# Joined maxima for two key chunks of the odd heads, in a one-core block of attention, feed-forward and linear attention

## The reference, cut to what matters

```python
x = x + attn_a(layernorm(x), ...)      # 2 sequences of 2048 tokens, 256 features
x = x + ffn(layernorm(x), ...)
x = x + attn_b(layernorm(x), ...)
x = x + ffn(layernorm(x), ...)

# attn_a: 16 query heads, 4 key/value heads of 16 features, full softmax
scores = jnp.einsum('bghnd,bhsd->bghns', q, k)
attn = jax.nn.softmax(scores / SCALE, axis=-1)
out = jnp.einsum('bghns,bhsd->bghnd', attn, v)
return out @ Wo + bo
```

## Time and profile before

| | |
|---|---|
| median of 3 runs | 2197.43 us (2196.96 to 2198.44) |
| the profiled execution's own time | 2189.54 us |
| its span | 2187.7 us |
| busy: PE, DVE, ACT, POOL | 95%, 82%, 68%, 6% |
| attention steps with maxima | about 149 to 1398 us of the span |
| mean granted PE clock | 0.973 of full speed |

### The profile page before, as it was taken

How to read it: one execution, slowest core, us unless ns; L and a number is a source line. 1 busy time by engine, 2 the same in 40 slices (tenths; PEclk the granted TensorE clock), 3 DMA queues, 4 the chain that set the end, 5 groups by cost and what they waited for, 6 DMA issues and landing times.

```text
span 2187.7 us, 48018 instructions
## 1 busy us (share of the span) xinstructions
PE 2085.6 (95%) x14214; PEld 857.4 (39%) x14214; DVE 1784.7 (82%) x3349; ACT 1478.1 (68%) x2899; POOL 140.7 (6%) x210
## 2 busy tenths in 40 slices
PE   6899999999999999999999999898997999998997
PEld 3423333333333333333333333254434555555433
DVE  5689999999999999999999999644537677776255
ACT  4438888888888888888888888744556434446653
POOL 2350000000000000000000000010002000002000
PEclk9779999999999999999999999999997999999998
DMA  6421121121121221221221221230000000000002
GB/s 165 129 69 42 45 74 48 48 75 42 52 72 41 56 68 41 62 63 41 63 61 41 66 58 42 74 102 26 1 0 1 1 0 1 1 0 1 0 0 77
DMA packets 93686, 101.19 MB, mean 46 GB/s; under 512 B 35712, under 2 KB 74896, under 8 KB 93552
## 3 DMA queue, kind: packets, MB, share of 16 engines
q1 hardware_dynamic: 93552, 99.79, 16.8%
HBM read 78.72 MB, written 20.71 MB: 45 GB/s over the span
## 4 chain that ended last, share of the span: by engine, by line
PE 86%; DVE 6%; issue 3%; ACT 3%; DMA 1%; SPq 0%; ACTq 0%; POOL 0%; DVEq 0%; POOLq 0%
PE ps L613 22%; PE ps L587 14%; PE ps L636 10%; PE ps L642 10%; PE ps L743 8%; PE ps L751 4%; PE ps L553 3%; PE ps L819 2%; PE ps L828 2%; PE ps L848 2%; PE ps L602 1%; ACT YT L1001 1%; PE ps L764 1%; PE ps L532 1%; PE ps L867 1%
## 5 line engine op out<-in xcount | busy, mean ns | idle before, releaser
L1298 DVE TENSOR_REDUCE mx<-ps 128x1 f32<-128x512 f32 x2048 | 1279.4, 683 | 23.5 <-PE ps L587 18.8
L1001 ACT ACTIVATE YT<-ps 128x512 f32<-128x512 f32 x2048 | 1058.0, 606 | 273.8 <-PE ps L642 273.7
L613 PE MATMUL ps<-YT,work 128*32 128x512 f32 x4096 | 546.1, 605 | 0.0
L587 PE MATMUL ps<-work 64*128 64x512 bf16 x2048 | 461.3, 389 | 7.5 <-DVE mx L1298 6.9
L636 PE MATMUL ps<-work 64*128 64x512 bf16 x2048 | 406.0, 378 | 2.8
L642 PE MATMUL ps<-work 34*128 34x512 bf16 x2048 | 400.6, 378 | 0.0
L587 PEld LDWEIGHTS ps<-work 64*128 64x128 bf16 x2048 | 144.6, 93 | 613.0 <-DVE mx L1298 541.6
L636 PEld LDWEIGHTS ps<-work 64*128 64x128 bf16 x2048 | 162.0, 94 | 110.5 <-ACT YT L1001 36.3
L743 PE MATMUL ps<-YT,c_s 128*128 128x512 f32 x384 | 176.6, 603 | 3.2 <-ACT work L1050 2.5
L613 PEld LDWEIGHTS ps<-YT,work 128*32 128x32 f32 x4096 | 80.7, 108 | 123.0 <-issue 86.9
L642 PEld LDWEIGHTS ps<-work 34*128 34x128 bf16 x2048 | 101.1, 94 | 49.6 <-issue 1.7
(11 more groups left out here) (142 smaller groups left out, 1670.2 us busy)
## 6 DMA issues: line engine op xcount, KB each, us to landing
work<-k_scr SPq DMA_DIRECT2D x640, 64.0 KB, 2.2
work<-q_scr SPq DMA_DIRECT2D x640, 32.0 KB, 1.8
o_scr<-o_sb SPq DMA_DIRECT2D x32, 256.0 KB, 2.1
X<-in_L_attn_a_x_dram SPq DMA_DIRECT2D x8, 512.0 KB, 7.3
work<-negt SPq DMA_DIRECT2D x256, 1.0 KB
work<-o_scr SPq DMA_DIRECT2D x16, 256.0 KB
work<-inv_scr SPq DMA_DIRECT2D x16, 256.0 KB
out_dram<-X SPq DMA_DIRECT2D x16, 256.0 KB, 2.2
```

The source lines that it names most:

```text
L587: mm(ps[:, bank_of[x], :], qa[rows, p, jp, qt * P:(qt + 1) * P], ka[rows, p, kc_ * CH:(kc_ + 1) * CH], start=True, stop=True).then_inc(a_m ...
L613: m = mm(ps[32 * j:32 * j + 32, 7, :], vst[:, p, t, :], prob(GROUP * t + j), start=t == 0, stop=t == KTILES - 1)
L1001: fn(prob(u), ps[:, S_BANK + u % S_RING, :], ACT.Exp, scale=HD ** -0.5).then_inc(exp_ok, 1)
L1298: dve.tensor_reduce(mx[:, p, at_:at_ + 1], ps[:, bank_of[x], :], AX_X, ALU.max).then_inc(a_max, 1)
```

## The change: the key chunks 2 and 3 of the odd half share one pass on VectorE

For the odd half the loaded keys hold, in place of chunk 2, the difference of chunk 2 and chunk 3 (formed from float32 projections, split again in a high and a middle part, kept in the new scratch `d_scr`). So product x % 8 == 5 gives the difference of the two chunks' scores, and x % 8 == 7 the scores of chunk 3. ScalarE takes the positive part of the difference (`raised`, a Relu from PSUM into `above`), and VectorE adds it to the scores of chunk 3 and takes the maximum in one instruction (`tensor_tensor_reduce`). A step then has 56 VectorE passes in place of 64, and 8 Relus on ScalarE. The number of PE products and their order stay. PE waits for a Relu (`a_up`) where the bank held a difference.

```diff
-REDUCED = MAXU + 1
+SHARE = 2 * KC
+JOINED = MAXU // SHARE
+REDUCED = MAXU - JOINED + 1
...
+            def is_raised(x):
+                return x % SHARE == SHARE - 3
+            def is_joined(x):
+                return x % SHARE == SHARE - 1
+            def reduced_to(x):
+                return x + 1 - (x + 3) // SHARE
...  # PE, max_mm
-                wait(pe, a_max, REDUCED * s + after_of[x])
+                last = after_of[x]
+                if last == -4:
+                    wait(pe, a_up, JOINED * s)
+                elif last < 0:
+                    wait(pe, a_max, REDUCED * s + 1 + last)
+                elif is_raised(last):
+                    pe.wait_ge(a_up, JOINED * s + last // SHARE + 1)
+                else:
+                    pe.wait_ge(a_max, REDUCED * s + max(reduced_to(last), 1))
...  # ACT, the new helper, its places in a step
+            def raised(s, x):
+                act.wait_ge(a_mm, MAXU * s + x + 1)
+                if x >= 2 * SHARE:
+                    act.wait_ge(a_max, REDUCED * s + reduced_to(x + 2 - 2 * SHARE))
+                else:
+                    wait(act, a_max, REDUCED * (s - 1) + reduced_to(x + 2 + MAXU - 2 * SHARE))
+                act.activation(above[:, x // SHARE % 2, :], ps[:, bank_of[x], :], ACT.Relu).then_inc(a_up, 1)
...
                 for t in range(KTILES):
+                    x = AHEAD + GROUP * t + 1
+                    if is_raised(x) and x < MAXU and ahead >= 1:
+                        raised(s + 1, x)
+                    if is_raised(x) and x >= MAXU and ahead >= 2:
+                        raised(s + 2, x - MAXU)
                     for j in range(GROUP):
...  # ACT, chunks 6 and 7, in place of the loop over them
+            high(6, 0)
+            raised(0, 5)
+            put_row(0, 7, 0)
+            high(6, 1)
+            put_row(0, 7, 1)
+            raised(0, 13)
+            high(6, 2)
+            raised(0, 21)
+            raised(0, 29)
+            middle(6)
+            high(7, 0)
+            raised(0, 37)
+            high(7, 1)
+            high(7, 2)
+            raised(0, 45)
+            raised(0, 53)
+            raised(0, 61)
+            raised(1, 5)
+            raised(1, 13)
+            middle(7)
...  # ACT, middle
+                if c % CPG == CPG - 1:
+                    act.wait_ge(p_df, c // CPG + 1)
+                    if c >= CPG:
+                        act.wait_ge(d_st[0], 16 * 2)
+                    act.copy(part_d[:, 0, :], k_diff[:]).then_inc(p_dh, 1)
                 act.wait_ge(p_res, c + 1)
...
                 act.copy(part(c, 1), qkf(c)).then_inc(p_mid, 1)
+                if c % CPG == CPG - 1:
+                    act.wait_ge(p_ds, c // CPG + 1)
+                    act.copy(part_d[:, 1, :], k_diff[:]).then_inc(p_dm, 1)
...  # SP, store: the stores of d_scr
+                if pt < 2 and c4 != 2:
+                    sp.dma_start(d_scr[b * KV_HEADS:(b + 1) * KV_HEADS, pt, :, ch(c4)],
+                                 part(c, pt)[0:64, 2, :]).then_inc(k_st[pt][buffer_of(c)], 16)
+                if pt == 1 and c4 == CPG - 1:
+                    sp.wait_ge(p_dm, b + 1)
+                    for r in range(2):
+                        sp.dma_start(d_scr[b * KV_HEADS:(b + 1) * KV_HEADS, r, :, ch(2)], part_d[:, r, :]).then_inc(d_st[b], 16)
...  # DVE, maxima
-                    dve.wait_ge(a_mm, MAXU * s + x + 1)
-                    dve.tensor_reduce(mx[:, p, at_:at_ + 1], ps[:, bank_of[x], :], AX_X, ALU.max).then_inc(a_max, 1)
+                    if is_raised(x):
+                        continue
+                    at_ = place(x)
+                    if not is_joined(x):
+                        dve.wait_ge(a_mm, MAXU * s + x + 1)
+                    if is_joined(x + 1):
+                        dve.wait_ge(a_mm, MAXU * s + x + 2)
+                        dve.wait_ge(a_up, JOINED * s + x // SHARE + 1)
+                    if is_joined(x):
+                        dve.tensor_tensor_reduce(out=joined[:], in0=ps[:, bank_of[x], :], in1=above[:, x // SHARE % 2, :],
+                                                 scale=1.0, scalar=LOWEST, op0=ALU.add, op1=ALU.max,
+                                                 accum_out=mx[:, p, at_:at_ + 1]).then_inc(a_max, 1)
+                    else:
+                        dve.tensor_reduce(mx[:, p, at_:at_ + 1], ps[:, bank_of[x], :], AX_X, ALU.max).then_inc(a_max, 1)
...  # residue of chunk 3 (DVE) and of chunk 7 (POOL), around its own subtraction
+                    pool.wait_ge(p_kd, 2)
+                    pool.tensor_tensor(k_diff[:], k_diff[:], qkf(c)[0:KVD, 2, :], ALU.subtract).then_inc(p_df, 1)
...
+                    pool.wait_ge(p_dh, 2)
+                    pool.wait_ge(p_res, NCH)
+                    pool.tensor_tensor(k_diff[:], k_diff[:], part_d[:, 0, :], ALU.subtract).then_inc(p_ds, 1)
```

More of the change, by code:

```diff
@@ L58 @@
 S_BANK, S_RING = 3, 4
+LOWEST = -3.0e38
 GLOBAL_AT = (5, 9)
@@ L169, in hybrid_block @@
         mx = sb("mx", [P, 2, MAXU])
+        joined = sb("joined", [P, CH])
+        k_diff = sb("k_diff", [KVD, CH])
+        part_d = sb("part_d", [KVD, 2, CH], BF16)
         mxq = sb("mxq", [P, GROUP * QT])
@@ L212, in hybrid_block @@
         ka, qa = take(2, SEQ, dt=BF16), take(2, JP, CH, dt=BF16)
+        above = take(2, CH)
         def prob(u):
@@ L267, in hybrid_block @@
         x_ld = [sem(f"x_ld{c}") for c in range(NCH)]
+        d_st = [sem(f"d_st{b}") for b in range(BATCH)]
         def ch(c):
@@ L274, in kv_of, with place @@
             return s // (CPG * KV_HEADS) * KV_HEADS + s % KV_HEADS
+        def is_raised(x):
[4 more added lines that the diff above has]
+            return x + 1 - (x + 3) // SHARE
+        def place(x):
+            return (x % 2 * JP * QT + x // 2 // KC) * KC + x // 2 % KC
         bank_of, after_of = [], []
@@ L281, in hybrid_block @@
             bank_of.append(b_)
-            after_of.append(used[b_] + 1)
+            after_of.append(used[b_])
             used[b_] = x_
@@ L300, in buffer_of, with keys_stored @@
             return c // CPG * 2 + c % 2
+        def keys_stored(pt, c):
+            return (1, 1, 2, 2)[c % CPG] if pt == 2 else (2, 2, 3, 4)[c % CPG]
         def stored(eng, pt, c):
@@ L362, in load_queries, with load_keys @@
                                          q_scr[s, 2 * jp + g, 0:2].rearrange("r d n -> (r d) n")).then_inc(done[p], 16)
-            def load_keys(k_dst, p, s, done):
+            def load_keys(k_dst, p, s, done, odd):
                 for g in range(2):
@@ L368, in load_keys, with load_coarse @@
                         for part_row in (row, row + HD):
-                            sp.dma_start(k_dst[part_row:part_row + HD, p], k_scr[kv_of(s), r]).then_inc(done[p], 16)
-            def load_coarse(q_dst, k_dst, p, s, done):
+                            sp.dma_start(k_dst[part_row:part_row + HD, p], (k_scr, odd)[g][kv_of(s), r]).then_inc(done[p], 16)
+            def load_coarse(q_dst, k_dst, p, s, done, odd):
                 load_queries(q_dst, p, s, done)
-                load_keys(k_dst, p, s, done)
+                load_keys(k_dst, p, s, done, odd)
             def load_fine(p, s, done):
@@ L431, in _ @@
                     stored(sp, pt, c)
+            sp.wait_ge(d_st[1], 16 * 2)
             def next_maxima(s, p):
@@ L958, in high @@
                 fn(qkf(c)[:, n, :], ps[:, qk_bank(c, n), :], ACT.Identity, bias=b)
+                if n == 2 and c % CPG == 2:
+                    wait(act, p_dm, c // CPG)
+                    fn(k_diff[:], ps[0:KVD, qk_bank(c, n), :], ACT.Identity, bias=bias[0:KVD, BK:BK + 1]).then_inc(p_kd, 1)
                 fn(part(c, 0)[:, n, :], ps[:, qk_bank(c, n), :], ACT.Identity, bias=b).then_inc(p_act, 1)
             def middle(c):
+                if c % CPG == CPG - 1:
[3 more added lines that the diff above has]
+                    act.copy(part_d[:, 0, :], k_diff[:]).then_inc(p_dh, 1)
                 act.wait_ge(p_res, c + 1)
@@ L991, in collect, with step @@
                 act.copy(o_sb[:, p, :], ps[:, 7, :]).then_inc(o_ev, 1)
-            def step(i, p, before=True):
+            def step(i, p, before=True, ahead=2):
                 s = 2 * i + p
                 for t in range(KTILES):
+                    x = AHEAD + GROUP * t + 1
[3 more added lines that the diff above has]
+                        raised(s + 2, x - MAXU)
                     for j in range(GROUP):
@@ L1008, in _ @@
             step(1, 1)
-            with act.Fori(2, STEPS // 2) as i:
+            with act.Fori(2, STEPS // 2 - 1) as i:
                 step(i, 0)
                 step(i, 1)
+            step(STEPS // 2 - 1, 0, ahead=1)
+            step(STEPS // 2 - 1, 1, ahead=0)
             collect(STEPS - 1, STEPS // 2 - 1, 1)
@@ L1233, in residue @@
                 dve.wait_ge(p_act, 3 * (c + 1))
+                if c == CPG - 1:
+                    dve.wait_ge(p_kd, 1)
```

(5 more changed lines are left out.)

24 lines of the change are left out of this document (15 added, 9 removed).

## The result

The changed kernel takes 2213.8 us (median of 4 runs, 2211.91 to 2214.37) against 2197.23 us (median of 4; three of them gave the 2197.43 of the table): ratio 1.0074, 95% interval 1.0059 to 1.009, so 16.6 us slower. The forecast was +26.8.

A forecast was written before the change was run, and what follows sets the result against it. It took a loop of latencies between PE and VectorE, 2.48 us a unit, to bound the kernel. Passes 0, joined pass 0, odd Relus 0, boundaries 10.8 and start 16.0 gave +26.8 us, 2224 us; range 2206 to 2262.

The forecast's parts named there:

- The loop of latencies: Attention units: 2.48 us set by waits between PE and VectorE, kept in every unit; removed passes return 0.
- 35 us: Attention units: gain if the fourth product were not held, 0.07 us a unit, 2.41 us each, over 31 steps x 16 units.
- The closing units don't gain either: Two units closing a step's maximum: no gain, as their fourth product waits in the same order as now.
- The joined pass: VectorE in odd units: the add-and-maximum pass takes 0.60 us, up to 0.71 free; cost 0, upper end 122 us.
- rival C: VectorE's joined pass is longer than 0.71 us: +22 us at 0.80, +122 at 1.20; chance 0.22.
- The Relu in odd units: ScalarE in odd units: the Relu takes 0.49 us, covered by existing waits; cost 0, upper end 12 us.
- Rival D: ScalarE's Relu switches activation tables: 657 us more, 2880 us in all; chance 0.01.
- The start: Before the first step: middle(7) behind raised(1, 13) delays PE's first fine product from 148.46 to 164.5; +16.0 us, bounds +11 to +20.
- the extra work of the earlier chunks: Before attention: chunk 3's extra stores and casts fall where ScalarE waits; cost 0, upper end 2 us.
- The boundaries: Steps 1 to 30: Relu behind ScalarE's copy of the sums, 0.33 us each, 0.40 with a loop turn; 10.8 us, bounds 0 to 15.
- A: Attention units: VectorE's pace is the bound, units go to 2.41 us, 2189 us or 2173; chance 0.06.
- B: Only the step boundaries or only the start cost as read: 2208 to 2214 us; chance 0.16.

The follow-up runs named there:

- Experiments 2 and 3: Kernel before, each unit's fourth reduction (2) or first reduction (3) over 16 of 512 keys: 2182.86 us (ratio 0.9964) and 2145.54 us (0.9783).
- experiment 2: Kernel before, with each unit's fourth reduction over 16 of the 512 keys, 512 passes in all: 2182.86 us, ratio 0.9964.
- experiment 1: Changed kernel with middle(7) put ahead of raised(0, 61) in ScalarE's order: 2199.64 us, ratio 1.0037 against the kernel before.
- experiment 4: Experiment 1 plus the Relu of x = 21, behind the copy of the sums, over 16 of 512 columns: 2190.29 us, ratio 0.9994 against the kernel before.
- experiment 5: Kernel before, with ScalarE's loop over the steps 4 to 31 written out, nothing else: 2179.93 us, ratio 0.9936.
- experiments 1, 5 and 6: 1 and 5 as listed; 6 is experiment 1 with ScalarE's loop written out: 2188.51 us, ratio 0.9979 against the kernel before.

## Why the prediction was right

It said slower, by 26.8 us in the profiled execution, 2224 by the runs; it is +22.4 profiled and +16.6 by the runs, inside the range. Which of the two is nearer the truth is not told by these runs: the profiled execution of before lies 7.7 us below its own median, the changed one 1.9, so part of the gap is scatter.

**The loop of latencies: right.** Units of 2.48 us in both kernels, with 115 us less VectorE work in 1000. Experiments 2 and 3 show the mechanism and not only the outcome: 512 fourth passes made short gave 9.2 us, as many first ones 46.5, and only the second moved the load of the fourth product. For 35 us I had worked out 0.07 a unit; it is 0.07 (2.48 to 2.41) on the trace, that is 35 of the 46.5. The trace places the rest, roughly: three units of each step lasted 2.57, 2.61 and 2.65 us before and last 2.41 there too, which is 0.36 us a step or 11 us beyond; the first fine product comes 4.2 us earlier; and the turns of ScalarE's loop cost some 3.5 us more (3.74 for 3.47). One point was too strict: "The closing units don't gain either". A lighter VectorE did shorten the second one by 0.16 in experiment 2. In the changed kernel it did not, as the prediction said: there no pass between the two was removed.

**The joined pass: right.** The next pass begins 0.62 us behind it, the addition of the earlier trace rows had 0.60, and up to 0.71 was free. The mean duration in the groups, 681 ns, is the same as a plain reduction's. So rival C is out. The rule of the Trainium skill on half throughput that the prediction quotes stays untested, since one source here came from PSUM.

**The Relu in odd units: right, and no table load.** 0.50 us to the next exponential, units unchanged. Rival D is out by this row of ScalarE's groups:
```profile
L1137 ACT ACT_TABLE_LOAD x2 | 2.6, 1283 | 3.1 <-PE ps L789 3.1
```
The count is that of the earlier trace rows, with 256 Relus more in the kernel. The trace agrees with the rule quoted from the Trainium skill (ScalarE: Activation LUTs, Table sets).

**The start: the right step, 16.0 forecast, 19.8 measured at the first fine product.** The chain itself came in the order written, but later from its first link on: the middle part's cast at 151.32 against 148.3 (+3.0), the loads of the negated maxima at 161.88 against 157.6 (+4.3; SyncE waited 3.1 us for the stores to land, not 2.2), the product at 168.29 against 164.5 (+3.8). The last link was read wrongly: the 1.57 us from the end of the loads to the product is no landing time, as before the change PE was busy with lone maxima products until 148.06. Here it is 168.29 - 167.22 = 1.07. The part that was mis-sized most is the one costed at "0, upper end 2": the extra work of the earlier chunks, of which the prediction names chunk 3's alone. VectorE's first reductions in the changed kernel:
```profile
90.32 1.76 DVE L1326 TENSOR_TENSOR qkf_b<-qkf_b,part_b 128x1536 f32<-128x1536 f32 x1 [7.01 <-ACT part_b L1008]
...
96.35 2.47 DVE L1404 TENSOR_REDUCE mx<-ps 128x1 f32<-128x512 f32 x4
```
and in the kernel before:
```profile
86.87 1.76 DVE L1234 TENSOR_TENSOR qkf_b<-qkf_b,part_b 128x1536 f32<-128x1536 f32 x1 [6.94 <-ACT part_b L959]
...
92.89 2.47 DVE L1298 TENSOR_REDUCE mx<-ps 128x1 f32<-128x512 f32 x4
```
They begin 3.46 us later, and so does what feeds them, 90.32 against 86.87: the delay was there before the attention began. It comes through ScalarE, which waits longer for the stores of the parts before it may go on. After:
```profile
57.77 0.69 ACT L1004 ACTIVATE work<-ps,bias 128x512 f32<-128x512 f32 x1 [5.40 <-DMA q_scr<-work]
```
and before:
```profile
55.51 0.69 ACT L958 ACTIVATE work<-ps,bias 128x512 f32<-128x512 f32 x1 [3.83 <-DMA q_scr<-work]
```
The wait is 5.40 us in place of 3.83, and ScalarE goes on 2.26 us later (57.77 against 55.51), of the 3.46. What it waits for is a store of chunk 1, and SyncE issues that one 2.26 us later too. After:
```profile
37.48 0.59 SPq L432 DMA_DIRECT2D d_scr<-work  x1
...
40.02 0.56 SPq L432 DMA_DIRECT2D d_scr<-work  x1
...
53.13 0.55 SPq L432 DMA_DIRECT2D d_scr<-work  x1
53.72 1.27 SPq L440 DMA_DIRECT2D q_scr<-work  x2
```
and before:
```profile
51.46 1.26 SPq L405 DMA_DIRECT2D q_scr<-work  x2
```
Three stores into `d_scr` stand ahead of it, 1.7 us in sum, and SyncE's first store of all was 0.57 us later already (36.73 against 36.16). They copy the keys of the chunks 0 and 1, which the prediction's sum has nowhere. The other 1.2 us fit chunk 3's difference (an evaluation and casts more on ScalarE), which no run took alone. The 3.46 are of one pair of executions. Over the four kept traces without the change the first reduction begins at 92.4 to 94.4 us, over the four with it at 93.3 to 97.7; the means differ by 2.6. This is also why experiment 1 returned 12.8 to 15 us and not 16 or more: of the 4.8 us that remain at its start, 2.7 are there when VectorE's first reductions begin (95.55 against 92.89).

**The boundaries: 10.8 forecast, about 4.5 measured.** From the end of step 0 (shift 18.6 us, as 1.2 returned on the way) to the first exponentials of step 31 (1431.23 against 1408.07, 23.2 us) the steps cost 4.5 us. The mechanism is shown by experiment 4, with a short Relu the unit falls to 2.49. The sizes, from the lengths of all units: without a turn 14 boundaries cost 0.29 us and the first three 0.20, in place of 0.33. With a turn the three units around it sum to 1.06 above 2.49, against 0.98 before, so 0.08 in place of 0.40: this is the term that was too large. The turn that is gone gives its 0.98 back, which I took as 0. 14 x 0.29 + 3 x 0.20 + 12 x 1.06 + 0.2 at the loop's end - 13 x 0.98 = 4.8, of which 4.5 is left where step 31 begins.

Why so little at a turn: ScalarE itself resumes sooner there. After:
```profile
822.02 2.06 ACT L1086 ACTIVATE YT<-ps 128x512 f32<-128x512 f32 x4 [0.86 <-PE ps L688]
```
The idle time at the turn is 0.86 us, in the earlier trace rows it was 1.57; over all turns the means are 0.83 and 1.57. The trace's records of ScalarE's sequencer, which runs ahead of the engine (the branch in step 15 of before stands at 797.71, and two exponentials begin at 798.04 and 798.52), say most of why. From the loop's branch to the next record pass 2.81 us in the mean before (797.71 to 800.53 in step 15) and 2.55 after (819.24 to 821.84). Of that, the exponentials already issued cover 1.43 us before (two still begin behind the branch) and 1.91 after (three), so 0.48 of the 0.74 us is one more exponential that runs while the sequencer turns. The turn itself is 0.26 shorter. In every turn of both kernels two packets of the DMA queue for instructions move in between, in step 15 before:
```profile
q14 instruction: 2, 0.02, 2.2%
```
The first of them starts 0.32 to 0.60 us behind the branch before and within 0.03 us of it after, which more than covers the 0.26. From 400 to 1380 us this kind has 63 packets before, 60 after and 18 in experiment 5, where the loop is written out and the idle time gone. So a turn goes with a fetch of the loop's instructions; why the fetch starts sooner after the change no run tells. Experiment 4 shows that the Relu behind the copy costs at the turns as well: without it their excess is 0.62, less than the 0.98 of the kernel before.

**The rivals.** A (VectorE's pace the bound) is out by experiments 2 and 3. It had its grain of truth in two places, the closing unit and the lone products at the start, where VectorE's pace does count. B (only one of the two terms) is closest in size, since the boundaries gave less than half, and 2213.8 lies at the end of its 2208 to 2214; both terms exist, though.

By its terms: 0 + 0 + 0 + 4.5 + 18.6, and 0.8 less from step 31 on (2.1 returned in it, 1.3 lost behind it), make the 22.4 us. That the sum came this near is in part luck: the start was 2.6 us larger than forecast and the boundaries 6.3 smaller.

## What to carry to other kernels

An engine that is 98% busy can still be off the path: look for idle time of 0.1 us inside one repeated unit and ask which of its passes the next product waits for. 512 passes shortened there gave 46.5 us, 512 others 9.2. Work put into an in-order queue is paid for by what stands behind it: one item moved three calls later cost some 13 us, and one extra instruction behind a copy 0.3 us each time. And look for the cost of a loop's own turn on every engine: writing one out gave 12.9 us, where the removed passes returned nothing.

## What the runs showed of the hardware that I had not expected

- A turn of ScalarE's loop lengthened one unit by 0.98 us (3.47 for 2.49) before. It took the sequencer 2.81 us from the branch to its next record, with two instruction packets moved in between, and cost the engine about the part that the work already issued did not cover: 1.57 us with two exponentials still to begin behind the branch, 0.83 with three (and a turn of 2.55).
- A reduction of the sum of two tensors, one from PSUM and one from SBUF, took VectorE no longer than a plain reduction (681 ns against 685), and the read of its accumulator, 0.08 us, lay beside its neighbours.
- The releaser that the trace names is no proof of a wait. The 0.84 us behind the value sums carries VectorE's name even where the passes are short, "issue" in other units of the same kernel, and is the sums' own duration in all.
- In 150 to 160 us the granted clock was 0.64 before (1.00 is the upper of its two levels, 2.4 GHz, and 0.50 the lower). After it was 0.50, and 0.50 in 160 to 170 as well, with PE busy 2.80 and 1.71 us of each 10; in 170 to 180 it was 0.78. Of the 19.8 us, 1.2 returned by the end of step 0 all the same, all of it in the first unit: from its value sums' load to the next unit's it took 157.82 - 153.86 = 3.96 us before and 176.45 - 173.63 = 2.82 after. The clock's record shows the difference: it went from 0.50 to 1.00 at 157.17 before, 3.3 us into that unit, and at 174.35 after, 0.7 us into it. In experiments 1, 5 and 6 the first unit has 1.2, 3.3 and 1.1 us at the lower level and takes 3.05, 3.95 and 2.99 us.
